# A one-block transformer kernel on one core: norm turns in another PSUM bank and at other places of TensorE's list, low weight parts on GpSimd

## What is computed

```python
attn_in = _adaln(x, cond, ln1_w, ln1_b, g1_w, g1_b, b1_w, b1_b)
x = _attn(attn_in, attn_in, sa_wq, sa_wkv, sa_wo, sa_bo) + x
cross_in = _adaln(x, cond, ln1_w, ln1_b, g1_w, g1_b, b1_w, b1_b)
ctx_n = _ln(context, ca_lnc_w, ca_lnc_b)
x = _attn(cross_in, ctx_n, ca_wq, ca_wkv, ca_wo, ca_bo) + x
ffn_in = _adaln(x, cond, ln2_w, ln2_b, g2_w, g2_b, b2_w, b2_b)
h = jax.nn.gelu(ffn_in @ ff_w1 + ff_b1, approximate=False)
x = h @ ff_w2 + ff_b2 + x
```

## Time and profile before

| | us |
|---|---|
| median of 3 runs | 1188.44 (1187.24 to 1192.88) |
| the profiled execution | 1189.7 |
| its span, first to last instruction | 1187.9 |

### The profile page before, as it was taken

How to read it: one execution, slowest core, us unless ns; L and a number is a source line. 1 busy time by engine, 2 the same in 40 slices (tenths; PEclk the granted TensorE clock), 3 DMA queues, 4 the chain that set the end, 5 groups by cost and what they waited for, 6 DMA issues and landing times.

```text
span 1187.9 us, 18656 instructions
## 1 busy us (share of the span) xinstructions
PE 1109.8 (93%) x6888; PEld 787.2 (66%) x6888; DVE 873.6 (74%) x1068; ACT 635.6 (54%) x893; POOL 717.4 (60%) x454
## 2 busy tenths in 40 slices
PE   3589999999999999989999999999999999885998
PEld 3366666676666667666666666666666666564997
DVE  1467887878788877877778877788788778755443
ACT  2346556565656555556765555555555555675321
POOL 1368677766676666578887666666666666773000
PEclk9789999999999999999999999999999999997999
DMA  5112112221112111201112111211121112110001
GB/s 173 36 36 73 37 37 50 55 66 29 48 30 72 36 37 36 68 23 32 37 46 59 34 34 35 64 32 34 36 68 37 37 36 63 28 37 1 19 18 36
DMA packets 65689, 52.36 MB, mean 44 GB/s; under 512 B 29120, under 2 KB 48576, under 8 KB 65344
## 3 DMA queue, kind: packets, MB, share of 16 engines
q1 hardware_dynamic: 63712, 49.59, 16.7%
q10 hardware_dynamic: 1888, 1.59, 0.4%
HBM read 15.22 MB, written 2.10 MB: 15 GB/s over the span
## 4 chain that ended last, share of the span: by engine, by line
PE 79%; DVE 11%; ACT 4%; issue 4%; POOL 1%; DMA 1%; SPq 0%; ACTq 0%; POOLq 0%; DVEq 0%
PE ps L759 16%; PE ps L621 12%; PE ps L623 10%; PE ps L622 10%; PE ps L747 5%; PE ps L737 5%; PE ps L712 4%; DVE neg_max L906 4%; PE ps L819 4%; PE ps L718 4%; PE ps L714 4%; PE ps L716 3%; DVE w_lo L893 2%; PE ps L634 1%; ACT z L440 1%
## 5 line engine op out<-in xcount | busy, mean ns | idle before, releaser
L482 ACT ACTIVATE probs<-ps 128x1024 f32<-128x1024 f32 x256 | 262.0, 1026 | 211.4 <-PE ps L718 189.6
L906 DVE TENSOR_REDUCE neg_max<-ps 128x2 f32<-128x1024 f32 x256 | 299.1, 1219 | 56.9 <-PE ps L737 56.9
L371 POOL TENSOR_TENSOR acc<-acc,probs 128x1024 f32<-128x1024 f32 x128 | 308.4, 2409 | 18.4 <-ACT probs L482 0.4
L759 PE MATMUL ps<-probs,v 128*64 128x512 f32 x1024 | 230.7, 592 | 0.0
L379 POOL TENSOR_TENSOR eo<-tmp 128x512 f32<-128x512 f32 x64 | 92.4, 1443 | 210.8 <-DVE tmp L932 207.3
L366 POOL TENSOR_TENSOR acc<-probs 128x1024 f32<-128x1024 f32 x64 | 152.9, 2389 | 85.8 <-ACT probs L482 85.7
L759 PEld LDWEIGHTS ps<-probs,v 128*64 128x64 f32 x1024 | 73.6, 137 | 145.7 <-issue 145.7
L932 DVE TENSOR_TENSOR tmp<-ps,rope 128x1024 f32<-128x1024 f32 x128 | 150.5, 1214 | 6.7 <-PE ps L623 6.6
L621 PE MATMUL ps<-xn_hi,w_hi 128*128 128x512 f32 x256 | 110.1, 430 | 12.8 <-issue 6.4
L737 PE MATMUL ps<-hi 64*128 64x512 f32 x512 | 109.8, 419 | 11.2 <-DVE neg_max L906 8.5
L712 PE MATMUL ps<-max_rows,pick 64*128 64x512 f32 x512 | 109.5, 420 | 0.4 <-ACT probs L482 0.2
(11 more groups left out here) (109 smaller groups left out, 2182.6 us busy)
## 6 DMA issues: line engine op xcount, KB each, us to landing
lo<-eo SPq DMA_DIRECT2D x512, 64.0 KB, 2.0
w_raw<-pack_dram SPq DMA_DIRECT2D x16, 192.0 KB, 3.3
x<-x_dram SPq DMA_DIRECT2D x4, 512.0 KB, 10.5
w_raw<-pack_dram SPq DMA_DIRECT2D x8, 256.0 KB, 4.0
max_rows<-neg_max SPq DMA_DIRECT2D x128, 2.0 KB, 2.0
w_raw<-w_dram SPq DMA_DIRECT2D x2, 1024.0 KB, 5.8
out<-x SPq DMA_DIRECT2D x4, 512.0 KB, 2.9
ctx_in<-ctx_dram SPq DMA_DIRECT2D x4, 384.0 KB, 3.5
```

Of the source, the lines that this page charges most:

```text
L371: pool.tensor_tensor(acc[:, g % 2, :, :], acc[:, g % 2, :, :], probs[:, i, :, :], ALU.add).then_inc(added, 1)
L482: act.activation(probs[:, i, :, :], score_ps(i), ACT.Exp, scale=SCALE).then_inc(exped, 1)
L759: mm = pe.matmul(av_ps[DH * h:DH * h + DH, :], v[:, u % 2, kt, c:c + DH], probs[:, kt, h, :], start=(kt == 0), stop=(kt == TT - 1))
L906: dve.tensor_reduce(neg_max[:, g % 2, :, i], peak_ps(i), AX.X, ALU.max, negate=True).then_inc(maxed, 1)
```

## The change

Six things change.

1. A norm turns into bank 2 (was 1) and 7, the last norm as before. PE's wait for the kept average ahead of the turn is gone, and the wait for the scaled first half goes from the first score of the next period to the second (`kt == 1`), which writes banks 2 and 3.
2. On PE the turn of a norm that is not "at once" stands ahead of `project(p + 4)`, that of one "at once" between `project_v(u + 1, 0)` and `(u + 1, 1)`. Both stood between `project` and the first of them.
3. On ACT, the scaling of a norm that is not at once comes whole ahead of both `keep_v`; of one at once, `keep_v(0)`, `norm(0)`, `keep_v(1)`, `norm(1)`. It was `norm(0)`, `keep_v(0)`, `norm(1)`, `keep_v(1)` for all.
4. ACT's `split_weights` stands behind `high_qk` instead of at the end of the period.
5. The low parts of the weights are made by POOL (`low_weights`), behind the third `add_probs` and ahead of `rotate`, instead of by DVE at the end of its period. The first set stays on DVE.
6. POOL's `add_bias` for norms of x stands in the period three behind the one with the statistics, ahead of `rotate`; it stood at the end of the period with the rows. For n = 1 to 3 that is 0, 2, 4, for 8 to 11 it is 30, 32, 34, 36, for 12 to 14 it is 62, 64, 66.

The rope table is turned through banks 5 and 6 instead of 1 and 2, with a wait ahead of the first `modulate` on PE.

```diff
@@ ln_ps @@
-            return ps[:, (6 if n == LAST else 1, 7)[r], :]
+            return ps[:, (6 if n == LAST else 2, 7)[r], :]
@@ tables @@
+        bias_in = {at[0] + 3: n for n, at in norm_at.items() if order[n][0] == X}
+        def low_weights(eng, w, m):
+            eng.wait_ge(w_high, 4 * w + m + 1)
+            if m < 2:
+                for kt in range(KT):
+                    c = slice(kt * D, (kt + 1) * D)
+                    split = eng.tensor_tensor(w_lo[:, m, c].rearrange("p (e a f) -> p e a f", e=2, a=4),
+                                              w_raw[:, m, c].rearrange("p (a e f) -> p e a f", e=2, a=4),
+                                              w_hi[:, m, c].rearrange("p (e a f) -> p e a f", e=2, a=4),
+                                              ALU.subtract)
+                split.then_inc(w_split, 1)
+            else:
+                eng.tensor_tensor(w_lo[:, m, :], w_raw[:, m, :], w_hi[:, m, :], ALU.subtract)\
+                   .then_inc(w_split, 1)
@@ POOL, period @@
+                if p in split_in:
+                    low_weights(pool, *split_in[p])
+                if p in bias_in:
+                    add_bias(bias_in[p])
                 if is_job(p + 4):
                     rotate(p + 4)
-                n = rows_in_period.get(p)
-                if n is not None and order[n][0] == X:
-                    add_bias(n)
@@ ACT, period @@
                 if is_pair(p + 2):
                     high_qk(p + 2)
+                if p in split_in:
+                    split_weights(*split_in[p])
...
+                turned = turned_in.get(p)
+                turned_late = turned is not None and norm_at[turned][3]
+                if turned is not None and not turned_late:
+                    norm(turned, 0)
+                    norm(turned, 1)
+                if p % 2 == 1 and is_quad(u + 1):
+                    keep_v(u + 1, 0)
+                if turned_late:
+                    norm(turned, 0)
+                if p % 2 == 1 and is_quad(u + 1):
+                    keep_v(u + 1, 1)
+                if turned_late:
+                    norm(turned, 1)
...
-                if p in split_in:
-                    split_weights(*split_in[p])
@@ PE, norm @@
-                    p = norm_at[n][2] if n in norm_at else -1
-                    if p > 0:
-                        pe.wait_ge(av_kept, min(p + 1, PAIRS))
@@ PE, score @@
-                    if g - 1 in turned_in:
-                        pe.wait_ge(ln_scaled, 2 * turned_in[g - 1] + 1)
+                if kt == 1 and g - 1 in turned_in:
+                    pe.wait_ge(ln_scaled, 2 * turned_in[g - 1] + 1)
@@ PE, period @@
+                n = turned_in.get(p)
+                at_once = n is not None and norm_at[n][3]
+                if n is not None and not at_once:
+                    norm(n, 0)
+                    norm(n, 1)
                 if is_job(p + 4):
                     project(p + 4)
-                n = turned_in.get(p)
-                if n is not None:
-                    norm(n, 0)
-                    norm(n, 1)
...
                 if p % 2 == 1 and is_quad(u + 1):
                     project_v(u + 1, 0)
+                if at_once:
+                    norm(n, 0)
+                    norm(n, 1)
+                if p % 2 == 1 and is_quad(u + 1):
                     project_v(u + 1, 1)
@@ PE, start @@
+            pe.wait_ge(rope_kept, 1)
             modulate(0)
```

More of the change, by code:

```diff
@@ L547, in period @@
                     guess_rstd(n)
-                keeps_v = p % 2 == 1 and is_quad(u + 1)
-                for r in range(2):
-                    if p in turned_in:
-                        norm(turned_in[p], r)
-                    if keeps_v:
-                        keep_v(u + 1, r)
+                turned = turned_in.get(p)
[11 more added lines that the diff above has]
+                    norm(turned, 1)
                 n = rows_in_period.get(p)
@@ L568, in _ @@
             act.wait_ge(rope_turned, 1)
-            act.copy(rope[:, :, :], ps[:, 1:3, :]).then_inc(rope_kept, 1)
+            act.copy(rope[:, :, :], ps[:, 5:7, :]).then_inc(rope_kept, 1)
             split_weights(0, 1)
@@ L615, in turn_rope @@
                     for tt in range(TT):
-                        mm = pe.transpose(ps[:, 1 + s, tt * 128:(tt + 1) * 128],
+                        mm = pe.transpose(ps[:, 5 + s, tt * 128:(tt + 1) * 128],
                                           eo[:, s, tt * 128:(tt + 1) * 128], ident[:, :])
@@ L886, in norm_stats @@
                 dve.tensor_scalar(var_eps[:, :], mean_var[:, :, 1], EPS, None, ALU.add).then_inc(ln_step, 1)
-            def split_weights(w, m):
-                dve.wait_ge(w_high, 4 * w + m + 1)
-                if m < 2:
-                    for kt in range(KT):
-                        c = slice(kt * D, (kt + 1) * D)
-                        split = dve.tensor_tensor(w_lo[:, m, c].rearrange("p (e a f) -> p e a f", e=2, a=4),
-                                                  w_raw[:, m, c].rearrange("p (a e f) -> p e a f", e=2, a=4),
-                                                  w_hi[:, m, c].rearrange("p (e a f) -> p e a f", e=2, a=4),
-                                                  ALU.subtract)
-                    split.then_inc(w_split, 1)
-                else:
-                    dve.tensor_tensor(w_lo[:, m, :], w_raw[:, m, :], w_hi[:, m, :], ALU.subtract)\
-                       .then_inc(w_split, 1)
             def peak(g, i):
@@ L980, in _ @@
             refine_rstd(dve, 0)
-            split_weights(0, 0)
-            split_weights(0, 1)
+            low_weights(dve, 0, 0)
+            low_weights(dve, 0, 1)
             modulate(0)
@@ L986, in _ @@
             modulate(1)
-            split_weights(0, 2)
-            split_weights(0, 3)
+            low_weights(dve, 0, 2)
+            low_weights(dve, 0, 3)
             for p in range(FIRST, PAIRS + 3):
```

## The result

The changed kernel takes 1172.13 us (median of 4 runs, 1171.53 to 1172.47). The kernel before, beside it on the same chip, took 1188.65 (1187.24 to 1192.88); the ratio of after to before is 0.9849, with a 95% interval of 0.9824 to 0.9874. That is 16.5 us faster where 26 were forecast: inside the range, at its far end. The profiled execution has a span of 1170.5 us, 17.4 less than before.

The account below looks back on a forecast made before the run. PE, busy 93% of the span, was taken to bound the kernel, through its list, stands and stretched matmuls. Gains 19.0 + 1.4 + 2.2 + 3.6 = 26.2 from 1189.7 gave 1163.5; median 1.3 lower, so 1162 us, range 1154 to 1173.

Parts of the forecast that it names:

- low parts to POOL, high parts to mid-period: Weight pieces of the 28 split periods: the SP stages' excess over 4.88 us is taken back, 19.0 us gained.
- Rival (a): DVE's low_qk waits for POOL's low_weights; 0.57 us lost after each of 14 even split periods, 1170; chance 0.12.
- (d): POOL's low_weights outlasts its cover in 14 odd split periods; each us above 6.0 costs 14, slower than before; chance 0.03.
- (e): SP stages stay late because their lateness has another cause: only 7.2 us gained, 1181; chance 0.02.
- norm 1: Period -3: with POOL's bias later, the low part that PE waits for ends earlier, 1.7 us gained.
- period 61: PE's 2.39 us wait and the half clock behind it go; less ACT's lateness, 2.7 us net, bounds 1.0 and 4.1.
- norms at once: Periods 27, 29, 31, 33: PE's stall of 1.47 us is filled with project_v(0); net 0.35 each, 1.4 together.
- the weights' 4.7: Part of the weights' gain: excess of the SP stages of periods 28, 29 and 34, 4.7 us together.
- norm 3: Listed under the later bias, ahead of the middle periods: gains 0.35 us, as each of the four norms at once.
- the end: Periods 61 and 63: PE's stalls there go, less what ACT and o_low delay; 3.6 us gained together.
- Rival (b): Norms at their lower bound, -1.0 us each, and 1.0 instead of 2.7 at the end: 1170.5; chance 0.10.
- norm 2: Listed under the later bias: gains only 0.2 us, since the next exp is bound by ACT.

Follow-up runs that it names:

- low_parts_thrice: The changed kernel with two more unused 128x512 subtractions on POOL behind each weight piece: 1188.97 us.
- low_on_dve: The changed kernel with the weights' low parts back on DVE at the end of its period, ACT's high parts still at mid-period: 1181.47 us.
- low_parts_and_bias: The kernel before with low parts on POOL, high parts at mid-period and the later bias for norms 1 to 3 and 8 to 11: 1172.82 us.
- turn_first: bias_end_back with the at-once turns directly behind project, ahead of both project_v halves, and ACT's scaling ahead of each keep_v: 1167.73 us.
- high_o_first: The changed kernel with ACT's rounding of the pair's output ahead of the norm's rows in periods of norms at once: 1165.33 us.
- bias_end_back: The changed kernel with the bias of norms 12 to 14 alone back at the end of the period of their rows: 1168.12 us.
- norms_alone: The changed kernel with low parts back on DVE, high parts and bias back at the end of the period: 1194.81 us.
- low_parts_twice: The changed kernel with one more unused 128x512 subtraction on POOL behind each weight piece: 1174.00 us.
- low_parts_alone: The kernel before with only the weights' low parts on POOL and ACT's high parts behind high_qk: 1173.99 us.

## Why the prediction was right or wrong

**Right: low parts to POOL, high parts to mid-period.** For the 24 periods outside the middle the sum gave 14.3, and 14.4 came, with the stages at 4.82 to 4.88, where it named 4.9. `low_weights`, bounded by 1.24 and 2.48 us a piece, takes 2 x 1.16 or 2.07 on the mean (groups of the changed kernel: busy us, mean ns of one, idle time before):
```profile
L272 POOL TENSOR_TENSOR w_lo<-w_raw,w_hi 128x256 fp32r<-128x256 f32 x28 | 31.9, 1160 | 0.0
L278 POOL TENSOR_TENSOR w_lo<-w_raw,w_hi 128x512 fp32r<-128x512 f32 x14 | 28.9, 2067 | 0.0
```
Rival (a), `low_qk` loses the lock in even periods, didn't come: the stages behind even split periods are not at 5.2. It is POOL that waits for `low_qk` there: the first half of a piece takes 1.73 us and the second 0.73, in periods 4 and 12 as in most others. Rivals (d) and (e) are out too; low_parts_thrice shows that (d) is real, though: two extra operations of 1.25 cost 16.8 us, from 1172.13 to the time before. By the step's slope of 14 us for each us above 6.0, a piece of 2.3 plus 2.5 should have cost nothing. The mechanism is another than a shift of `rotate`: DVE behind POOL's unbroken row.

The Trainium skill (GPSIMD Engine Reference, 3.1 Elementwise — side-by-side cycle accounting) would keep such work on VectorE, since it takes 1.96 times as long on GpSimd. A piece of two halves did take longer on POOL, 2.3 against 1.8 in low_on_dve's rows (0.73 for a half that waits for nobody, against 0.41 on DVE in the kernel before), and moving it gained 9.3 us all the same.

**Right: norm 1 and period 61.** Norm 1's low part was to gain 1.7, and 1.8 came; low_parts_and_bias shows that it is the bias. PE goes on at 50.29 instead of 53.66, 1.1 sooner than named; 1.0 of that is the start-up, whose length differs between executions: the first `project` begins at 30.8 to 32.2 in the fourteen traces. Period 61 was to give 2.7, and 2.8 came. The clock stays at full speed there (timeline of PE at the start of period -2, then the window from the turn in 61):
```profile
50.29 0.77 PE L644 MATMUL ps<-xn_hi,w_hi 128*128 128x512 f32 x1 [4.26 <-issue]
```
```profile
1009.40:1022.50 13.10, 13.10 (x93) 1.00 0.02 2
```

**Wrong in one term: norms at once.** The step said 0.35 each, 1.4 for four: 1.5 of stall filled, less 0.75 for the late exp, less 0.4 for `low_qk` behind the third add. The first two are right: stages 28, 30, 32 and 34 take 5.53 to 5.54, where 5.6 was named, and turn_first, whose scalings come earlier, has 4.85 to 4.88 there. The third term failed. It saw that `low_qk` would wait for the add, but counted the delay only against the maxima on DVE, and sized it from period 32, where ACT and POOL were already late. It overlooked two things: that ACT, coming early to `high_qk`, would wait for transfers (a wait that stood in the earlier trace rows with 6.5 us and grew to 18.5), and that PE's first maximum needs the bank that `add_out` reads. The stages that follow, 29, 31, 33 and 35, take 6.03 to 6.26, 1.3 above the undisturbed 4.88 and not 0.4. If the weights' 4.7 is counted as won, the four norms came to -1.2 (3.5 measured in periods 27 to 35); by terms, the filled 6.0 less 4 x 0.65 less 4 x 1.3 is -1.8, so 0.6 is not placed. high_o_first, which cuts this chain at ACT, is 6.8 us faster; its trace has 5.2 less in periods 27 to 35 and 3.1 less in 0 to 3.

The split of the 3.5 depends on the order, and that is a second fault of the step: it added two terms that share POOL. Weights and later bias without the turns gave 2.1, or 3.6 with the 1.5 of clock put back, so that the turns on top are worth 1.4 or -0.1. In either order 2.6 of the 6.1 forecast is missing.

**Wrong in sign: norm 3.** It was put with the four, +0.35; periods 1 to 3 lost 2.3, and 1.6 of that is a loss of clock that other traces of the same lists don't have. The same chain runs there, but PE stands 1.51 at once, and then the clock is granted at 0.59 in the next 4 us (timeline, then window):
```profile
119.51 0.62 PE L757 MATMUL ps<-hi 64*128 64x512 f32 x2 [1.51 <-DVE x L953]
```
```profile
119.50:123.50 4.00, 3.99 (x20) 0.59 0.26 63
```
4.0 x 0.41 = 1.6, on top of the 1.51. In low_parts_thrice and in bias_end_back, whose lists are the same up to there, PE stands 1.47 and 1.37 in this stage at full clock, and it takes 6.73 and 6.24. In high_o_first stage 3 takes 4.9.

**Wrong in sign: the end.** For period 63 I reckoned 0.9 gained and for the bias nothing: "fits POOL's idle time of 3.43". That is the idle time of period 24; in periods 64 and 66 DVE does two-input work beside POOL, and no row of those periods was read for this step. It cost 1.2 and 1.8 instead. bias_end_back has 20.7 in the first of the two stretches where the kernel before has 21.6, just the 0.9 of the forecast; so the chain was read rightly, and the term that was put at nothing, the bias, cost 2.1 there and up to 3.0 behind it.

**Rival (b)**, norms at their lower bound, named 1170.5 and is nearest to what happened, but by another split, which is luck: it gave each of the four norms -1.0 where -0.3 came, period 61 only 1.0 where 2.8 came, and left period 63 its gain of 0.9 where 3.0 was lost by the end.

The numbers then close: 26.2 forecast, less 2.6 (four norms), 2.6 (norm 3), 2.1 and 1.8 (the end), plus 1.0 (start-up), is 18.1, against 17.4 in the span. The rest is norm 2: it was to gain 0.2, and period 0 takes 0.65 more, with a stage of 5.53 instead of 4.88.

## What to carry to other kernels

Filling one engine's stall makes every other engine late by what was filled, so follow each of them around the loop until it meets a wait that has slack, and count every buffer for which the filled engine waits, not only the busiest producer. Cost a moved operation in the very periods in which it lands, the last ones above all, where other work lies beside it. A slower engine is the better place for an operation if its idle time lies there and the faster engine's does not, as long as its row keeps gaps. And before a difference of 1 or 2 us between two traces is credited to an edit, read the granted clock of the stretch that it sits in.

## What the runs showed of the hardware

**The shared access is not lost for one operation only.** A two-input operation on DVE that meets POOL at work mostly got in at the next boundary between two of POOL's operations: of the boundaries less than 0.1 us wide that `low_qk` and the weights' subtractions met in the fourteen traces, they took some 350 and passed about ten. But these can come in rows: `low_qk` passed five boundaries in low_parts_thrice (8.93 us for 1.31) and the weights' pair at least one in norms_alone (5.05 us for 1.03). The Trainium skill (SBUF — State Buffer, SBUF: two separate sides) has the access as an exclusive lock held for a whole instruction, which these rows bear out; who gets it when POOL's next operation is already waiting, no run here settles.

**A step of 128x4 can cost as much as POOL's whole operation**: 2.30 us on DVE (L249, at 1070.98) beside the bias. The same step takes 0.16 at the start of the kernel before (L248, at 18.41).

**The same stand is not always followed by half clock.** In the changed kernel the stand of 1.51 us in period 3 was, and that cost 1.6 us more. In low_on_dve PE stands 1.46 us in the same stage, which takes 6.71 in all, so 5.25 besides, at a granted clock of 1.00. At this place a stand of 1.47 was followed by a clock of 0.58 over 4 us in low_parts_twice and of 1.00 in low_parts_thrice, though both kernels have done the same until then. Ahead of the turn in period 33, a stand of 1.62 was followed by 0.69 in low_parts_and_bias and by 1.00 in low_parts_alone, and the longest stands there, 1.92 (low_parts_alone, period 29) and 2.30 (low_parts_and_bias, period 1), by 1.00. So the length of the stand does not decide it by itself, and these rows don't tell what does. It matters when runs are compared: one such loss is 1.5 us, as much as all four new turns seemed to be worth.
